# Layer norm factors of a six-stage decoder: the reciprocal root as one power on GpSimd

## The reference, cut to what matters

```python
def _layernorm(x, axis=-1, eps=1e-05):
    m = jnp.mean(x, axis=axis, keepdims=True)
    v = jnp.var(x, axis=axis, keepdims=True)
    return (x - m) / jnp.sqrt(v + eps)
...
x = _layernorm(x + _L0_attn_ref(x, ...), axis=-1)            # bidirectional state space mixer
x = _layernorm(x + _L0_xattn_ref(x, ctx_1024, ...), axis=-1) # cross attention
x = _layernorm(x + _L0_ffn_ref(x, ...), axis=-1)             # quantised feed-forward
x = _layernorm(x + _L1_attn_ref(x, ...), axis=-1)            # causal self-attention
x = _layernorm(x + _L1_xattn_ref(ctx_1024, x, ...), axis=-1) # recurrent decoder, 128 steps
x = _layernorm(x + _L1_ffn_ref(x, ...), axis=-1)             # routed feed-forward, signed weights
```

## Time and profile before

| what | value |
|---|---|
| median of three runs | 4060.58 us |
| profiled execution | 4058.55 us, span 4056.8 us |
| PE busy | 3261.3 us (80%) |
| DVE busy | 2232.7 us (55%) |
| ACT busy | 1577.2 us (39%) |
| POOL busy | 505.4 us (12%), 1854 instructions |
| `up`, us 438 to 527 | PE 42.46, DVE 70.86, POOL 51.67 of 89 us |
| `yy`, us 3590 to 3690 | PE 43.30, DVE 73.35, POOL 57.36 of 100 us |

### The profile page before, as it was taken

The page is one execution under the profiler, slowest core; times in us unless marked ns, Lnnn a source line. Parts: engine busy times, 40 slices in busy tenths (PEclk is TensorE's granted clock), DMA queues, the critical chain, the costliest instruction groups (busy, mean ns, idle before and its releaser), DMA issues. The chain is left out here.

```text
span 4056.8 us, 109059 instructions
## 1 busy us (share of the span) xinstructions
PE 3261.3 (80%) x43050; PEld 2192.1 (54%) x43122; DVE 2232.7 (55%) x5373; ACT 1577.2 (39%) x3966; POOL 505.4 (12%) x1854
## 2 busy tenths in 40 slices
PE   7556568544489999998598999999999999965998
PEld 4424145322266666666354666666666666623554
DVE  2656767588845555555213555555555555563444
ACT  2221134344422222222112666666666666622222
POOL 0000421233300000000000000000000000033222
PEclk8576689877789999999798999999999999975888
DMA  2000020200010000000101333333333333301000
GB/s 95 3 3 0 10 46 9 86 0 0 0 44 0 0 0 0 0 0 0 52 26 50 90 90 90 90 90 88 91 89 90 90 90 87 93 18 48 25 26 31
DMA packets 278734, 176.56 MB, mean 44 GB/s; under 512 B 14320, under 2 KB 267840, under 8 KB 278608
## 3 DMA queue, kind: packets, MB, share of 16 engines
q1 hardware_dynamic: 275920, 172.57, 14.5%
q0 software_dynamic: 2752, 3.18, 0.5%
HBM read 164.98 MB, written 13.90 MB: 44 GB/s over the span
## 5 line engine op out<-in xcount | busy, mean ns | idle before, releaser
L1828 PE MATMUL ps<-de_hg,st_at 128*32 128x128 f32 x16384 | 516.3, 275 | 0.3 <-DVE st_at L1990 0.3
L1828 PEld LDWEIGHTS ps<-de_hg,st_at 128*32 128x32 f32 x16384 | 424.5, 110 | 31.6 <-DVE st_at L1990 0.5
L1893 ACT ACTIVATE st_th<-ps,st_sw 128x128 f32<-128x128 f32 x1024 | 292.8, 369 | 248.0 <-PE ps L1800 248.0
L1973 DVE TENSOR_TENSOR st_th<-ps,st_sw 128x512 f32<-128x512 f32 x256 | 177.2, 692 | 155.1 <-PE ps L1800 155.1
L1247 PEld LDWEIGHTS ps<-sa_xt,w_wq 128*128 128x128 f32 x2048 | 234.7, 194 | 11.1 <-issue 9.3
L1247 PE MATMUL ps<-sa_xt,w_wq 128*128 128x128 f32 x2048 | 237.9, 278 | 2.0 <-ACT sa_xt L1363 2.0
L1766 POOL COPY de_ah<-st_at 128x8 f32 (+1 forms) x256 | 51.1, 199 | 1507.0 <-DVE st_at L1990 1507.0
L1318 PE MATMUL ps<-sa_wo,sa_ct 128*128 128x512 f32 x512 | 225.0, 598 | 13.1 <-issue 13.1
L1789 PE MATMUL ps<-st_hk,st_cwt 112*32 112x128 f32 x4096 | 164.7, 278 | 84.9 <-DMA st_hk<-padded_alignments 82.9
L2228 PE MATMUL ps<-rf_wb,rf_sp 128*128 128x512 bf16 x737 | 202.2, 434 | 4.7 <-issue 2.9
L1800 PE MATMUL ps<-st_fs,st_waf 32*128 32x128 f32 x4096 | 186.5, 296 | 12.2
(11 more groups left out here) (410 smaller groups left out, 6456.5 us busy)
## 6 DMA issues: line engine op xcount, KB each, us to landing
st_hk<-padded_alignments SPq DMA_DIRECT2D x254, 448.0 KB, 3.6
X<-in_x_dram SPq DMA_DIRECT2D x16, 512.0 KB, 9.2
out_dram<-X SPq DMA_DIRECT2D x16, 512.0 KB, 2.7
w_wq<-in_Wq_perm_dram SPq DMA_DIRECT2D x1, 4096.0 KB
sa_wo<-in_Wo_perm_dram SPq DMA_DIRECT2D x1, 4096.0 KB, 14.2
gate_inputs<-dp_ro SPq DMA_DIRECT2D x16, 256.0 KB, 2.3
st_rin<-gate_inputs SPq DMA_DIRECT2D x128, 32.0 KB, 3.3
rf_wf<-in_weightT_dram SPq DMA_DIRECT2D x8, 512.0 KB, 4.3
```

Source lines behind the costliest of these rows:

```text
L1828: ins = pe.matmul(R[g][32 * q:32 * q + 32, :], at[g][:, b, :], hg[:, BG * g + b, q * P:(q + 1) * P], start=False, stop=(b == BG - 1), tile ...
L1893: ins = act.activation(th[g][:, b, :], sums(g, 0)[:, b // 2, (b % 2) * P:(b % 2 + 1) * P], ACT.Tanh, bias=sw[g][:, b:b + 1])
L1973: dve.tensor_tensor(th[g][:, 4:8, :].rearrange("p (k s) n -> p k s n", s=2), sums(g, 1).rearrange("p k (s n) -> p k s n", s=2), sw[g][:, 4 ...
```

## The change

The estimate on VectorE and the Newton steps go. `statistics` ends with `bn_aggr`, which raises `agg_done` itself; the wait for `bn_aggr` and the five instructions behind it are gone, so a tile has 2 links on VectorE in place of 7. `factors` on GpSimd waits for `agg_done` and has four instructions: minus the mean (not linked), variance plus epsilon (linked), the power -0.5 of that (linked), and the product of the two factors. `start_pool` fills three constants in place of one, each linked. `Norm` is used by all six stages; elsewhere only the bases of the semaphore counts change (`POOL_SETUP` in place of 1, and the new `POOL_LINKS`).

```diff
-        self.vy = t.sb("vy", [P, 2, 4])
-        self.c15 = t.sb("c15", [P, 1])
+        self.vy = t.sb("vy", [P, 2, 2])
+        self.consts = t.sb("consts", [P, 3])
...
-    LINKS = 7
-    POOL_LINKS = 12
+    LINKS = 2
+    POOL_LINKS = 2
+    POOL_SETUP = 3
 
     def start_pool(self, pool, link):
-        link(pool.memset(self.c15[:, :], 1.5))
+        for n, value in enumerate((LN_EPS, -0.5, -1.0)):
+            link(pool.memset(self.consts[:, n:n + 1], value))
...
         dve.memset(self.pad[:, k:k + 1], 0.0)
-        link(dve.bn_aggr(self.agg[:, k, :], self.stats[:, k, :, :]))
-        v, y, nm = self.vy[:, k, 0:1], self.vy[:, k, 1:2], self.vy[:, k, 3:4]
-        link(dve.tensor_scalar(v, self.agg[:, k, 1:2], LN_EPS, None, ALU.add))
-
-        link(dve.tensor_scalar(y.bitcast(I32), v.bitcast(I32), 1, None, ALU.logical_shift_right))
-        link(dve.tensor_scalar(y.bitcast(I32), y.bitcast(I32), -1.0, float(0x5F3759DF), ALU.mult, ALU.add))
-        link(dve.tensor_scalar(v, v, -0.5, None, ALU.mult))
-        dve.tensor_scalar(nm, self.agg[:, k, 0:1], -1.0, None, ALU.mult).then_inc(self.var_done, 1)
+        dve.bn_aggr(self.agg[:, k, :], self.stats[:, k, :, :]).then_inc(self.agg_done, 1)
 
     def factors(self, pool, link, b, k):
 
-        pool.wait_ge(self.var_done, b + 1)
-        v, y, q, nm = (self.vy[:, k, n:n + 1] for n in range(4))
-        for step in range(3):
-            link(pool.tensor_tensor(q, y, y, ALU.mult))
-            link(pool.tensor_tensor(q, q, v, ALU.mult))
-            link(pool.tensor_tensor(q, q, self.c15[:, :], ALU.add))
-            link(pool.tensor_tensor(self.rs[:, k, 0:1] if step == 2 else y, y, q, ALU.mult))
+        pool.wait_ge(self.agg_done, b + 1)
+        eps, power, minus = (self.consts[:, n:n + 1] for n in range(3))
+        v, nm = self.vy[:, k, 0:1], self.vy[:, k, 1:2]
+        pool.tensor_tensor(nm, self.agg[:, k, 0:1], minus, ALU.mult)
+        link(pool.tensor_tensor(v, self.agg[:, k, 1:2], eps, ALU.add))
+        link(pool.tensor_tensor(self.rs[:, k, 0:1], v, power, ALU.pow))
         pool.tensor_tensor(self.rs[:, k, 1:2], nm, self.rs[:, k, 0:1], ALU.mult).then_inc(self.rstd_done, 1)
```

More of the change, by code:

```diff
@@ L74, in __init__ @@
         self.rs = t.sb("rs_ln", [P, 2, 2])
-        self.vy = t.sb("vy", [P, 2, 4])
-        self.c15 = t.sb("c15", [P, 1])
+        self.vy = t.sb("vy", [P, 2, 2])
+        self.consts = t.sb("consts", [P, 3])
         self.pad = t.sb("pad", [P, 2])
-        self.var_done, self.rstd_done, self.row_free = t.sems("var_done rstd_done row_free")
-    LINKS = 7
-    POOL_LINKS = 12
+        self.agg_done, self.rstd_done, self.row_free = t.sems("agg_done rstd_done row_free")
+    LINKS = 2
+    POOL_LINKS = 2
+    POOL_SETUP = 3
     def start_pool(self, pool, link):
-        link(pool.memset(self.c15[:, :], 1.5))
+        for n, value in enumerate((LN_EPS, -0.5, -1.0)):
+            link(pool.memset(self.consts[:, n:n + 1], value))
     def start(self, act):
@@ L551, in _ @@
                     with pool.Fori(0, NB // 2) as i:
-                        link = Chain(pool, pool_seq, 1 + i * 2 * ln.POOL_LINKS)
+                        link = Chain(pool, pool_seq, ln.POOL_SETUP + i * 2 * ln.POOL_LINKS)
                         for k in range(2):
@@ L945, in _ @@
                         smooth(2 * i + 4 + k, k)
-                link = Chain(pool, pool_seq, 1 + (NB - 4) * ln.POOL_LINKS)
+                link = Chain(pool, pool_seq, ln.POOL_SETUP + (NB - 4) * ln.POOL_LINKS)
                 for b in range(NB - 4, NB):
@@ L1223, in _ @@
                         ln.factors(pool, link, 2 * i + k, k)
-                link = Chain(pool, pool_seq, 1 + (NB - 2) * ln.POOL_LINKS)
+                link = Chain(pool, pool_seq, ln.POOL_SETUP + (NB - 2) * ln.POOL_LINKS)
                 ln.factors(pool, link, LAST - 1, 0)
```

## The result

The changed kernel took 3990.8 us (median of 4 runs, 3988.7 to 3994.4) against 4062.3 us for the kernel before (4058.7 to 4066.2) on the same chip: a ratio of 0.9825, 95% interval 0.9808 to 0.9842, some 71 us less. The prediction was 3994 us.

> The changed kernel once more, unaltered. It tells the change's effect from what differs between two executions of one kernel. By stage the first traces gave a gain of 20.2 us for up, 22.4 for ca, 1.7 for ff, 1.3 for sa, 22.5 for the decoder with yy, and a loss of 1.6 in rf; the summed prediction, with the power's measured 0.55 us, was about 20, 16, 3, 3, 20 and 3.

What follows compares the result with a forecast made beforehand. VectorE's own time and, close behind, the row-buffer loop set the pace in `up` and `yy`. 17.4 + 17.4 + 13.2 + 20.3 - 1.0 = 67.3 us less 6e gave 66.1 us saved: 3994 us, range 3980 to 4040.

Steps and rivals of the forecast that it cites:

- What bounds the kernel: VectorE, closely followed by the row-buffer loop, paces `up` and `yy`; the norm is on the path in `ca` too.
- The power's price: GpSimd's power instruction in every norm: 0.2 us over an ordinary step's 0.19 us, with 0 and 3.7 as bounds.
- e: What the power on GpSimd takes over the 0.19 us of an ordinary 128x1 step; taken as 0.2 us.
- `up` and `yy`: Tiles fall from 5.55 to 4.39 us and from 5.64 to 4.48 us, saving 17.4 us in each stage.
- The six ends: Last norm of each stage, bare before a barrier: 3.39 - e us saved each, 20.3 - 6e together.
- `ca`: 14 of the 15 tiles with another behind them save the whole 0.94 us of VectorE time: 13.2 us.
- `ff`, `sa`, `rf`: No gain in these loops, since TensorE hides the norm; the L1094 wait grows from 0.35 to 1.29 us.
- The fills: Two more GpSimd constant fills at stage start, 0.16 us each, cost 1.0 us over `ff`, `sa` and `rf`.
- The lock: In `up` and `yy`, a power over 0.85 us shuts out VectorE's two-input instruction, costing 30 x (e - 0.65) us.
- the other reading: Without the lock for the power, the buffer loop alone bounds a long one: 15 x (e - 0.93) us, paying to e = 3.9.
- The long power: Rival, chance 0.15: power holds L594 and L2111 each tile; saving gone at 2.6 us, 4073 or 4107 us beyond.
- The first power: Rival, chance 0.03: GpSimd's first power is late once by a whole old period, costing 3.6 us: 3998 us.

Runs made afterwards that it cites:

- the two runs in which one limit alone was lifted: Changed kernel with the five VectorE instructions back, power kept: 4038.3 us; changed kernel with three Newton steps on GpSimd for the power, no estimate: 4037.6 us.
- the two second executions: The kernel before and the changed kernel, each run once more unaltered: 4050.9 us and 3985.4 us.
- 20 columns: Changed kernel with the power taken over 20 columns, of which one is used: 4025.6 us, ratio 0.9917.

## Why the prediction was right

**What bounds the kernel:** right, and confirmed from both sides by the two runs in which one limit alone was lifted. `up` and `yy` are VectorE's and, close behind, the buffer loop's. One row was misread, without consequence: the product of 3.45 us wasn't wholly at the lower clock (0.57 on average over it). At the lower clock it takes 3.78 us, still below 4.39.

**The power's price,** the largest unknown, was 0.55 us, e = 0.36 in place of the 0.2 taken. The bounds of 0 and 3.7 held it. The reasoning behind the choice got weak support: one more column costs (1.64 - 0.55) / 7 = 0.156 us, far over the 2.3 ns that a product over 1024 columns takes for a step of all lanes. A power is some 70 such steps. The assumption of 50 to 100 gave 0.1 to 0.2 us for it, which agrees; the other 0.2 us are a fixed part that the assumption lacked. How the lanes are served the runs don't tell: some 4 steps for each of 16 lanes in turn would cost as much.

**`up` and `yy`:** 4.51 and 4.54 us against 4.39 and 4.48. The step that failed is the 0.09 us between a tile's `bn_aggr` and the next row. It holds in every second tile; in the others VectorE's loop turns, and the gap is 0.37 us with nothing to wait for. Before, the longer wait for ScalarE covered it. That made the two terms 15 x 1.04 = 15.6 and 15 x 1.10 = 16.5 in place of 17.4 each.

**The six ends:** 3.17 us each, 19.0 in all, where 3.39 - 0.2 gave 19.1. Two errors cancel: the power was 0.16 us longer, and the first step isn't linked, so the second follows it after 0.14 us in place of 0.27.

**`ca`:** the mechanism was right and the term too small. Its loop gave 15 x 0.93 = 14.0 us for the 13.2 summed, and the end its 3.2. What the sum lacked is the clock: three tiles 1.4 us longer before, 4.2 us. With these it makes 21.4 of the 22.4 us measured (21.2 between the two second executions). The rows for it were in the trace of before, which has 15.80 us beside 14.40, but I had read a single tile.

**`ff`, `sa`, `rf`:** no gain in the loops, as forecast. In `ff` the wait before the gate's first instruction was 9.5 us over 16 tiles and is 22.4 us after, 0.81 us more a tile where 0.94 was expected; the pace stays at 20.5 us a tile. The work that went was handed to the wait for TensorE. Before and after:

```profile
  PE ps L961: 9.5, 16
```
```profile
L1086 DVE SCALAR_TENSOR_TENSOR ff_gu<-ps,ff_sc,ff_swg x16: 750/751/751, 767.0 to 1067.3; 128x512 f32<-128x512 f32 x16
its engine sat idle before it (us, times) until:
  PE ps L953: 22.4, 16
```

In the middle tiles the wait is 1.14 to 1.16 us, as it had been 0.34 and 0.21 by turns: the prediction had read one tile of the larger kind. In `sa` the idle time that the earlier trace rows show as 4.97 us became 5.91.

```profile
1480.99 2.29 DVE L1438 TENSOR_REDUCE sa_mx<-ps 128x16 f32<-128x2048 f32 x1 [5.91 <-PE ps L1273]
```

**The fills:** GpSimd's first copy in `sa` starts 0.47 us after the first fill, where it was 0.16: 0.31 us, as forecast. That the program pays this three times can't be told from scatter.

**The sum again,** with what was measured: 15.6 + 16.5 + 14.0 + 4.2 + 19.0 - 1.0 = 68.3 us, against 66.9 between the two profiled spans and 71 to 73 between the medians. The forecast's 66.1 differ from it by two loops that were taken 2.7 us too high, one that was 0.8 too low and a clock of 4.2 that was left out. That these nearly cancel is luck; the parts were right to 4.2 us.

**The lock** is the part that was wrong, though it moved nothing at 0.55 us. I had concluded from two pairs of rows (the 1.05 and 2.09 us of the earlier trace rows) that any GpSimd instruction shuts VectorE's two-input one out while it runs. The Trainium skill, page SBUF - State Buffer, section "Who interferes with whom", says that the lock is held for the whole instruction; for the power the trace doesn't bear this out, with L588 at 1.23 us inside 3.52 us. So the sign would not have changed at 2.6 us. The prediction had priced the other reading, the buffer loop alone, with a zero at e = 3.9. With 20 columns e is 3.34, where that reading leaves 67.3 - 6 x 3.34 - 15 x (3.34 - 0.93) = 11 us; measured were 36. The room of 0.93 us in it contradicts the 1.9 us that the prediction itself had worked out for the loop in `up`; with 1.9 it is 26. The long power was thus priced too high by either reading.

**The first power** wasn't late. In the first tile of `up`, `bn_aggr` ends at 433.47 us and the apply follows 1.44 us later; in the tile shown above it is 443.98 - 442.55 = 1.43.

```profile
433.97 0.55 POOL L108 TENSOR_TENSOR up_rs_ln<-up_vy,up_consts 128x1 f32<-128x1 f32 x1
434.59 0.19 POOL L109 TENSOR_TENSOR up_rs_ln<-up_vy,up_rs_ln 128x1 f32<-128x1 f32 x1
434.91 1.24 ACT L113 ACTIVATE X<-up_row,up_rs_ln 128x1024 f32 x1 [18.73 <-POOL up_rs_ln L109]
```

The cost of a first call which the Trainium skill names (page GPSIMD Engine Reference, section "2.1 Instruction dispatch") doesn't show here.

## What to carry to other kernels

Where two limits of nearly the same length share a pace, here VectorE's own work and the loop over two row buffers, a change is worth its time only if it shortens both; test each half alone before dropping one, and look that the half which is left in hasn't grown. Read the wait behind an instruction in every stage that runs it: 96 equal norms gave 1.1 us, 0.93 us or nothing a tile, and 3.2 us wherever a barrier bares the last one. When an engine comes free by such a change, give it a pass of the engine that now sets the pace.

## What the runs showed of the hardware

A power of a tensor by a tensor on GpSimd takes 0.55 us for 128x1, 1.64 for 128x8 and 3.53 for 128x20, so about 0.4 us and 0.156 us a column. An ordinary step of 128x1 takes 0.19 us.

A running power doesn't hold VectorE's addition of two tiles in SBUF (1.23 us inside 3.52), but a 128x1 product of GpSimd that starts inside that addition is held to its end (0.52 and 1.15 us in place of 0.19). GpSimd's add over 128x1024 beside VectorE's statistics and beside a pass with one operand in PSUM costs neither anything (1.42 and 1.22 us). The one case of the reverse stays that of the earlier trace rows; why the power differs from those products wasn't tried.

A TensorE idle time of 1.67 and of 1.9 to 2.1 us by turns in the tiles of `ca` came with a drop of the granted clock to 0.50 for some 3 us in two or three of the first 14 tile intervals; with 0.68 and 1.05 us there was none. In `up` the clock stayed at 1.00 with 1.5 us of idle time before each product of 1.98 us, and fell again and again with 2.4 to 2.7 us. A VectorE instruction count is thus also paid in TensorE's clock.
